# Float32 second matmuls for the first batch's experts and the last pass, and later, narrower splits of the expert weights

## What is computed

```python
logits = xf @ gate_w + gate_b
top_w, top_i = jax.lax.top_k(logits, K)                      # K = 2 of E = 8
...
for e in range(E):
    h = jax.nn.gelu(xf @ w1[e] + b1[e], approximate=False)   # 128 -> 512
    out = out + combine[:, e:e + 1] * (h @ w2[e] + b2[e])    # 512 -> 128
shared = jax.nn.gelu(xf @ ws1 + bs1, approximate=False) @ ws2 + bs2
...
x = x + jnp.tanh(g_ffn[0]) * (out + shared)
```

## Time and profile before

| | us |
|---|---|
| median of 3 runs | 161.34 (161.28 to 161.44) |
| the profiled execution, its own time | 162.54 |
| its span, first to last instruction | 160.7 |
| busy: PE / DVE / ACT / POOL | 139.1 / 122.2 / 117.8 / 122.2 |
| attention units 0 to 23, h of pass 0 starts | at 95.13 |
| y of the last pass starts, ends | at 156.40, 157.91 |

### The profile page before, as it was taken

The page is one execution under the profiler, slowest core; times in us unless marked ns, Lnnn a source line. Parts: engine busy times, 40 slices in busy tenths (PEclk is TensorE's granted clock), DMA queues, the critical chain, the costliest instruction groups (busy, mean ns, idle before and its releaser), DMA issues.

```text
span 160.7 us, 4634 instructions
## 1 busy us (share of the span) xinstructions
PE 139.1 (87%) x1916; PEld 104.4 (65%) x1916; DVE 122.2 (76%) x223; ACT 117.8 (73%) x192; POOL 122.2 (76%) x95
## 2 busy tenths in 40 slices
PE   7669789799879997888989789978799996999962
PEld 4423544257547555566767679866798995999962
DVE  1867898678897999997776156999979963966591
ACT  3444789999877894969896989499257786878730
POOL 5504799799999999696878968555598899886850
PEclk9987999999999999999999999999999999999999
DMA  4589970360030000000000000000000001000001
GB/s 146 182 278 264 300 228 0 91 174 4 4 130 2 4 0 4 0 0 4 4 0 4 0 4 4 0 0 4 0 2 4 2 4 33 0 4 0 4 0 33
DMA packets 10254, 7.73 MB, mean 48 GB/s; under 512 B 1101, under 2 KB 8442, under 8 KB 10234
## 3 DMA queue, kind: packets, MB, share of 16 engines
q1 hardware_dynamic: 10234, 7.44, 15.3%
HBM read 7.18 MB, written 0.26 MB: 46 GB/s over the span
## 4 chain that ended last, share of the span: by engine, by line
PE 48%; DVE 24%; ACT 14%; issue 6%; DMA 3%; POOL 1%; SPq 1%; DVEq 0%; ACTq 0%; POOLq 0%
PE banks L989 10%; PE banks L991 9%; PE banks L990 9%; DVE part L809 9%; DVE wf L913 6%; ACT prob L704 4%; DMA ring<-in_L_xattn_Wq_dram 3%; ACT prob L637 3%; PE banks L1168 3%; PE banks L1118 2%; PE banks L1170 2%; PE banks L1169 2%; DVE k_both L792 2%; ACT v_hi L626 2%; PE banks L1136 2%
## 5 line engine op out<-in xcount | busy, mean ns | idle before, releaser
L536 POOL TENSOR_TENSOR p_lo<-prob,p_hi 128x1024 f16<-128x1024 f32 x23 | 51.4, 2244 | 6.9 <-ACT p_hi L645 6.9
L558 POOL TENSOR_TENSOR k_both<-prob,k_both 128x1024 f16<-128x1024 f32 (+1 forms) x18 | 37.3, 2077 | 12.3 <-DVE k_both L927 9.5
L704 ACT ACTIVATE prob<-banks,b1T 128x256 f32<-128x256 f32 x72 | 28.3, 481 | 10.5 <-PE banks L991 8.6
L809 DVE TENSOR_REDUCE part<-banks 128x2 f32<-128x1024 f32 (+1 forms) x24 | 29.0, 1215 | 2.0 <-PE banks L1086 1.1
L637 ACT ACTIVATE prob<-banks 128x1024 f32<-128x1024 f32 x24 | 24.5, 1021 | 7.0 <-PE banks L1136 6.9
L989 PE MATMUL banks<-wf,k_both 128*128 128x128 f16 x144 | 25.1, 220 | 4.2 <-POOL k_both L558 2.9
L927 DVE CAST k_both<-prob 128x512 f16<-128x512 f32 (+1 forms) x18 | 19.5, 1085 | 8.8 <-ACT prob L704 8.8
L645 ACT ACTIVATE p_hi<-prob 128x1024 f16<-128x1024 f32 x24 | 25.4, 1057 | 0.8
L990 PE MATMUL banks<-wf,k_both 128*128 128x128 f16 x144 | 25.0, 219 | 0.0
L991 PE MATMUL banks<-wf,k_both 128*128 128x128 f16 x144 | 25.0, 219 | 0.0
L989 PE MATMUL banks<-x2h,wf 128*128 128x256 f16 x72 | 19.6, 273 | 0.0
(11 more groups left out here) (152 smaller groups left out, 333.6 us busy)
## 6 DMA issues: line engine op xcount, KB each, us to landing
ring<-in_L_ffn_w_dram SPq DMA_DIRECT2D x16, 256.0 KB, 4.3
wf<-in_ctx_dram SPq DMA_DIRECT2D x2, 256.0 KB, 5.3
ring<-in_L_xattn_Wk_dram SPq DMA_DIRECT2D x2, 256.0 KB, 4.4
ring<-in_L_xattn_Wv_dram SPq DMA_DIRECT2D x2, 256.0 KB, 7.5
ring<-in_L_ffn_ws_dram SPq DMA_DIRECT2D x2, 256.0 KB, 6.9
x_sb<-in_x_dram SPq DMA_DIRECT2D x1, 256.0 KB, 2.9
ring<-in_L_xattn_Wq_dram SPq DMA_DIRECT2D x1, 256.0 KB, 5.3
ring<-in_L_xattn_Wo_dram SPq DMA_DIRECT2D x1, 256.0 KB, 8.0
```

Of the source, the lines that this page charges most:

```text
L536: nc.gpsimd.tensor_tensor(p_lo[:, u % RINGP, :, :].rearrange("p a n -> p (a n)"), prob[:, u % RINGE, :], p_hi[:, u % RINGP, :, :].rearrang ...
L558: nc.gpsimd.tensor_tensor(hid_lo[:, k % HB, cols], hid[:, k % 2, cols], hid_hi[:, k % HB, cols], ALU.subtract).then_inc(hl_done, 1)
L704: nc.scalar.activation(hid[:, k % 2, c * T1:(c + 1) * T1], span(2 * (k % 2), HC * T1)[:, c * T1:(c + 1) * T1], ACT.Gelu, bias=b1T[:, e * H ...
L809: nc.vector.tensor_reduce(dst, src, AX_X, ALU.max).then_inc(part_done, 1)
```

## The change

- For the passes in FULL32 (0 to 8 and 17) the hidden layer is not split, and y is 8 float32 matmuls of 128 columns, with `hid` as the stationary and w2, straight from `ring`, as the moving operand. It waits for the GELU and the load alone. `hid` gets three buffers, and each is free when y has read it.
- w2 isn't scaled there, so a second set of combine weights, `comb_g`, is made by one more small ACT instruction for each batch. (Slot 3 holds ws2 scaled in place, so pass 0 keeps `comb_s`.)
- For j = 2 to 4 the early split is of w1 alone, 128x512, on both POOL and DVE. w1 of j = 5 to 8 is split in steps 24, 25, 28 and 29 (W1_STEP), w2 of j = 2 to 8 in steps 26, 27 and 30 to 34 (W2_STEP), by ACT, and by DVE one step later.
- The passes 9 to 16 keep the split of the hidden layer as it was for k from 7 on: high part half by DVE, half by ACT, low part by POOL.
- Slots 3 and 4 are loaded again when y of pass 0 and of pass 1 is done.

```diff
+W1_STEP = {5: FFN0, 6: FFN0 + 1, 7: FFN0 + 4, 8: FFN0 + 5}
+W2_STEP = {2: FFN0 + 2, 3: FFN0 + 3, 4: FFN0 + 6, 5: FFN0 + 7, 6: FFN0 + 8, 7: FFN0 + 9, 8: FFN0 + 10}
...
+NHID = 3
+
+FULL32 = [*range(NE), NF - 1]
+SPLIT_HID = [k for k in range(NF) if k not in FULL32]
...
-        hid = prob[:, 0:2, :]
+        hid = prob
...
+        def early_part(j):
+
+            return 2 if j < 2 else 1
...
-                elif j == RING:
-                    sp.wait_ge(e_lo, 1)
-                elif j > RING:
-                    sp.wait_ge(ed_lo, j - RING)
+                elif j >= RING:
+                    sp.wait_ge(y_ps, j - RING + 1)
...
+                nc.scalar.activation(comb_g[:, tiles, :], comb[:, tiles, :], ACT.Identity,
+                                     scale=gates[:, 3:4]).then_inc(comb_ready, 1)
...
+                    elif k - NHID in FULL32:
+                        act.wait_ge(y_ps, k - NHID + 1)
                     else:
-                        act.wait_ge(hl_done, k - 1)
-                        if shared(k - 1) > 0:
-                            act.wait_ge(hd_done, shared(k - 1))
+                        act.wait_ge(hl_done, hid_splits(k - NHID))
...
                     e = EORDER[k % NE]
-                    pe.wait_ge(hl_done, k + 1)
+                    if k in FULL32:
+                        pe.wait_ge(ld_f[k % NE], 32)
+                        pe.wait_ge(gelu_done, HC * (k + 1))
+                    else:
+                        if k % NE in W2_LATE:
+                            pe.wait_ge(w2_lo, W2_LATE.index(k % NE) + 1)
+                        pe.wait_ge(hl_done, hid_splits(k))
                     if k >= 2:
                         pe.wait_ge(y_done, QT * (k - 1))
                     for q in range(QT):
                         for c in range(HC):
...
+                            if k in FULL32:
+                                last = nc.tensor.matmul(banks[:, 4 + k % 2, q * D:(q + 1) * D],
+                                                        hid[:, k % NHID, at:at + P], ring_f(k % NE)[:, 1, cols],
+                                                        start=(c == 0), stop=(c == HC - 1))
+                                continue
```

More of the change, by code:

```diff
@@ L179, with hid_splits @@
 HB = 3
[L181 to L199, removed]
+NHID = 3
+FULL32 = [*range(NE), NF - 1]
+SPLIT_HID = [k for k in range(NF) if k not in FULL32]
+def hid_splits(k):
+    return sum(1 for m in SPLIT_HID if m <= k)
 def plan_misc():
@@ L295, in block_kernel @@
         comb_s = sb("comb_s", [P, NT, NE], F32)
+        comb_g = sb("comb_g", [P, NT, NE], F32)
         combT = cT[0:NE, 0, :].bitcast(F32)
@@ L360, in block_kernel @@
         hh_act = sem("hh_act")
-        f_hi, f_lo = sem("f_hi"), sem("f_lo")
+        w1_hi, w1_lo = sem("w1_hi"), sem("w1_lo")
+        w2_hi, w2_lo = sem("w2_hi"), sem("w2_lo")
         h_ps = sem("h_ps")
@@ L551, in _ @@
                 k = i - FFN0 - 1
[L552 to L558, removed]
+                if k in SPLIT_HID:
+                    pool.wait_ge(hh_done, hid_splits(k))
+                    pool.wait_ge(hh_act, hid_splits(k))
+                    nc.gpsimd.tensor_tensor(hid_lo[:, k % HB, :], hid[:, k % NHID, :], hid_hi[:, k % HB, :],
                                             ALU.subtract).then_inc(hl_done, 1)
@@ L711, in _ @@
                         cols = slice(HC // 2 * T1, HC * T1)
[L712 to L716, removed]
+                        nc.scalar.activation(hid_hi[:, k % HB, cols], hid[:, k % NHID, cols], ACT.Copy).then_inc(hh_act, 1)
+                for j in W1_LATE:
+                    if W1_STEP[j] == i:
+                        act.wait_ge(ld_f[j], 32)
+                        nc.scalar.activation(wf[:, 0, EORDER[j], 0, :], ring_f(j)[:, 0, :], ACT.Copy,
+                                             scale=S_W).then_inc(w1_hi, 1)
+                for j in W2_LATE:
+                    if W2_STEP[j] == i:
+                        act.wait_ge(ld_f[j], 32)
+                        nc.scalar.activation(wf[:, 0, EORDER[j], 1, :], ring_f(j)[:, 1, :], ACT.Copy,
+                                             scale=S_W).then_inc(w2_hi, 1)
         @block.vector
@@ L963, in _ @@
                     if k % NE == 0:
-                        dve.wait_ge(comb_ready, b + 1)
+                        dve.wait_ge(comb_ready, 2 * (b + 1))
+                    weight = comb_g if k in FULL32 and k % NE > 0 else comb_s
                     for t in range(QT):
@@ L969, in _ @@
                             out=acc[:, QT * b + t, :], in0=banks[:, 4 + k % 2, t * D:(t + 1) * D],
-                            scalar=comb_s[:, QT * b + t, e:e + 1], in1=acc[:, QT * b + t, :],
+                            scalar=weight[:, QT * b + t, e:e + 1], in1=acc[:, QT * b + t, :],
                             op0=ALU.mult, op1=ALU.add).then_inc(y_done, 1)
@@ L974, in _ @@
                     dve.wait_ge(e_hi, j + 1)
[L975 to L979, removed]
+                    expert_lo(j, slice(0, early_part(j))).then_inc(ed_lo, 1)
+                for j in W1_LATE:
+                    if W1_STEP[j] == i - 1:
+                        dve.wait_ge(w1_hi, W1_LATE.index(j) + 1)
+                        expert_lo(j, slice(0, 1)).then_inc(w1_lo, 1)
+                for j in W2_LATE:
+                    if W2_STEP[j] == i - 1:
+                        dve.wait_ge(w2_hi, W2_LATE.index(j) + 1)
+                        expert_lo(j, slice(1, 2)).then_inc(w2_lo, 1)
                 if i == BIAS_STEP:
```

49 lines of the change are left out of this document (20 added, 29 removed).

## The result

The changed kernel takes **157.42 us** (median of 4 runs, 157.16 to 157.62), the kernel before, beside it, 161.37 (161.28 to 161.44): a ratio of 0.9755, with a 95% interval of 0.9737 to 0.9772. The forecast was 157.3, in a range of 156.0 to 160.0.

A forecast was written before the change was run, and what follows sets the result against it. No engine was taken to bound the whole: POOL and DVE were busy nearly throughout the attention, TensorE in the mixture. Terms +4.4 - 6.5 - 1.9 = -4.0 took 161.34 to 157.3 us, range 156.0 to 160.0.

The forecast's parts named there:

- Part 1: Mixture, on TensorE: ten passes with a float32 y at 0.111 us a record cost +4.4 us (bounds +3.4 and +12.2).
- Part 2: Mixture: TensorE's waits go, 5.5 us, and their pipeline drains, 1.0 us; together -6.5 us.
- All six: PE's waits from 95 to 158 us: four for POOL's low part (2.9 us), `qo` (1.4), `acc` (1.2).
- What I priced at nothing: Mixture: late loads of slots 3 and 4, `comb_g`, late w2 splits, ACT's work in steps 33 and 34; no cost.
- Part 3: Attention: half-width early splits at j = 2 to 4 shorten DVE's work or its waiting for POOL; -1.9 us.
- The gain of 1.4 at j = 3: Attention, 57.27 us: DVE's low part comes 0.05 us before POOL's `p_lo`, so `v_lo` ends earlier; 1.4 us gained.
- the 0.5 of j = 4: Attention: DVE's low part still waits for POOL's `p_lo` but gains its half width, 0.5 us, passed on to the scores.
- Gain 0: Attention, j = 2, 51.42 us: POOL's next `p_lo` starts first, so DVE's low part ends at 53.1 as before; 0 us.
- POOL first: Rival, attention, 57.3 us: POOL's `p_lo` starts before DVE, so the attention gives 0.5, not 1.9; 158.7 us, chance 0.22.
- New waits in the mixture: Rival, mixture: ACT's queue, late slots or DVE's weight halves bring two waits of 1 us; 159.3 us, chance 0.16.
- A record at 0.16, or a falling clock: Rival, float32 y: load and stream don't overlap fully (+12.2, 165.1 us), or the granted clock falls; chance of either 0.12.
- Cheap float32: Rival, float32 y: records stream at float16's 0.056 us, so y takes 0.9 us; 149 us, chance 0.03.

## Why the prediction was right, point by point

- **Part 1, the float32 y.** Taken at 0.111 a record: measured 0.1117 in the eight passes whose y follows directly on an h (matmuls of 256 columns), 0.117 in the first, behind matmuls of 65 columns, and 0.115 in the last, behind some of 128. Why those two are dearer isn't shown. Ten passes cost 1.87 + 8 x 1.79 + 1.84 = 18.0 us against 10 x 1.34: +4.6 where +4.4 stood. The experiment with more float32 found the same 0.45 a pass. The Trainium skill (TensorE: Matmul & The Clock Gate, Weight-path perf modes and LDWEIGHTS) gives float32 no fast weight load and a load a time of columns / 1.2, which for 128 columns is 107 ns, an estimate from that page. The trace agrees in kind, with 0.1117. Yet that the load sets this price isn't shown: 0.1117 is also twice the 0.056 at which float16 matmuls of 128 columns follow one another.
- **Part 2, the waits.** All six went. In -2.07 = +4.6 - 6.7 the last figure, which is only what remains, answers to the -6.5. `qo` is done at 106.60 us, 1.6 before TensorE takes it, and no engine waits for the late loads. What I priced at nothing cost nothing, but for one: y of pass 16 starts at 149.19 us where y of pass 15 has ended at 148.91, and its low part by POOL, done at 149.09, is what it waits for. 0.28 us; in the kernel before a like gap (0.24) was there and cost nothing, since the last y waited for DVE's `acc` anyway.
- **Part 3, the attention.** The moment of DVE's and POOL's instructions came out as worked out, when 1.39 us are added to the times of the changed kernel for the earlier start: j = 2 ends at 51.70 + 1.39 = 53.09 (53.1), j = 3 starts at 57.33 with POOL at 57.38 (57.3, 57.38), v_lo ends at 59.21 (59.2), h of pass 0 starts at 93.20 (93.2). The gain of 1.4 at j = 3 was measured as 1.40, which leaves 0.53 for the 0.5 of j = 4. Only the attribution was loose. "Gain 0" for j = 2 is what the rows show, yet the run with j = 2 alone at full width loses 1.5 us, most of it ahead of j = 3. Once the splits of j = 3 and 4 are narrow, the half widths of j = 2 are what keeps DVE, and the scores behind it, from falling behind, and the gain at j = 3 rests on them.
- **The rivals.** *POOL first*: not in the changed kernel, nor in the nine other profiles that keep the narrow splits. In all ten DVE's instruction at j = 3 takes 0.68 us and starts 0.05 to 0.06 us ahead of POOL's, so the lead is thin but steady. With j = 2 at full width POOL does come first, but most of that loss has another place, so that 158.95 beside the rival's 158.7 is luck; its price at j = 3 alone is untested. *New waits in the mixture*: only the 0.28 us in the changed kernel, but more in those with less float32, 0.2 to 0.4 us each. *A record at 0.16, or a falling clock*: 0.1117 and 1.00. *Cheap float32*: no. The Trainium skill (Perfetto Trace Analysis, Engine Utilization) puts float32 in its two-part form at half the output rate; here a float32 matmul of 128x128 takes two records, 0.223 us, against 0.056 for a float16 one: a quarter of the rate. The measurement decides.

DVE's waits for POOL are what the Trainium skill (SBUF — State Buffer, Who interferes with whom) says of two inputs in SBUF and an exclusive lock. The trace agrees in both directions: DVE's 512 columns take 0.68 us when it is first and 1.55 to 2.14 when it is second, POOL's `p_lo` 2.13 and 2.62.

## What to carry to other kernels

A dearer form of an operation on the bounding engine pays where it removes a wait of that engine that is longer than its surcharge: list that engine's waits, find what stands ahead of each, and change little else (here ten float32 passes gave 2.1 us in the mixture, five or six of them 3.2). Where two engines lock each other out, a busy time says little: subtract the other's end from one's own to get the true cost, and then ask who comes first: the gain at j = 3 stands on a lead of 0.05 us. And an experiment that gives the expected time can still lose it in another place, so look where each distance grows.

## What the runs showed of the hardware

- Float32 matmul records with 128 rows and 128 moving columns follow one another in 0.1117 us behind matmuls of 256 columns, at a granted clock of 1.00, though each load's row lasts 192 ns, so that the rows of the loads overlap one another.
- A wait of 0.28 us can stand in no list: the last record of y of pass 15 starts at 148.85 us, could be followed at 148.91 and is followed at 149.19, but its row ends only at 149.07, and the list of PE's waits is empty. The distance of starts shows it.
